# A graph-attention edge pass: the two weighted rows of a tile summed by an accumulating transfer instead of on VectorE

## The reference

```
xl = x @ Wl + bl;  xr = x @ Wr + br
e = leaky_relu(xl[src] + xr[dst], 0.2);  logits = sum over a head of e * att
m = segment_max(logits, dst);  p = exp(logits - m[dst]);  s = segment_sum(p, dst)
out = segment_sum(xl[src] * (p / s[dst]), dst) + bias      # self loops are added to src, dst
```

## Time and profile before

| | |
|---|---|
| device time, median of 3 | 3344.33 us |
| profiled execution: device time, span | 3327.99 us, 3326.3 us |
| busy in the span: PE, DVE, ACT, POOL | 82%, 85%, 51%, 25% |
| L732 of tile 0 to L677 of tile 75, pass 0 | 558.42 to 1105.00 us |
| mean granted TensorE clock | 0.916 of 2.4 GHz |

### The profile page before, as it was taken

How to read it: one execution, slowest core, us unless ns; L and a number is a source line. 1 busy time by engine, 2 the same in 40 slices (tenths; PEclk the granted TensorE clock), 3 DMA queues, 4 the chain that set the end, 5 groups by cost and what they waited for, 6 DMA issues and landing times. The chain is left out here.

```text
span 3326.3 us, 41230 instructions
## 1 busy us (share of the span) xinstructions
PE 2743.9 (82%) x11205; PEld 1838.8 (55%) x11205; DVE 2818.5 (85%) x5994; ACT 1689.0 (51%) x4291; POOL 844.1 (25%) x741
## 2 busy tenths in 40 slices
PE   7999997777777199999977777771899999688886
PEld 5777774333333078888843333330688888555554
DVE  7999996999999566767759999995988887399999
ACT  4545552555555433333315555553778787144443
POOL 0022212333332033333333333321333332000000
PEclk8999998889888589999988898885899999899998
DMA  9989997444443288887754444433999997388886
GB/s 322 344 300 318 319 335 268 133 153 150 152 154 121 72 271 274 271 266 261 251 198 142 150 152 155 149 105 131 379 357 351 350 345 269 129 292 287 293 291 226
DMA packets 332178, 788.76 MB, mean 237 GB/s; under 512 B 55070, under 2 KB 55616, under 8 KB 321738
## 3 DMA queue, kind: packets, MB, share of 16 engines
q1 hardware_dynamic: 265464, 622.14, 53.7%
q0 software_dynamic: 64032, 160.18, 15.1%
q10 hardware_dynamic: 2452, 3.79, 0.3%
HBM read 510.62 MB, written 329.28 MB: 253 GB/s over the span
## 5 line engine op out<-in xcount | busy, mean ns | idle before, releaser
L862 PE MATMUL bank<-wr,nT_e 128*128 128x512 f32 x1280 | 690.0, 689 | 241.7 <-ACT nT_e L662 241.4
L862 PEld LDWEIGHTS bank<-wr,nT_e 128*128 128x128 f32 x1280 | 268.5, 221 | 561.2 <-issue 292.3
L1019 PE MATMUL bank<-whi,t_hi 128*128 128x512 f32 x1256 | 525.1, 418 | 24.3 <-DVE t_lo L405 24.3
L1021 PE MATMUL bank<-whi,t_lo 128*128 128x512 f32 x1256 | 499.3, 398 | 0.0
L1020 PE MATMUL bank<-wlo,t_hi 128*128 128x512 f32 x1256 | 499.1, 397 | 0.0
L640 POOL DMA_INDIRECT nv_e<-rows,dst_row x160 | 255.6, 1598 | 701.8 <-ACT w_e L680 563.7
L677 ACT ACTIVATE w_e<-vs_e,ex_e 128x128 f32<-128x128 f32 x640 | 204.3, 390 | 336.3 <-DVE acc_e L794 251.6
L1019 PEld LDWEIGHTS bank<-whi,t_hi 128*128 128x128 f32 x1256 | 238.0, 189 | 74.6 <-issue 17.8
L1021 PEld LDWEIGHTS bank<-whi,t_lo 128*128 128x128 f32 x1256 | 238.1, 190 | 59.0
L1020 PEld LDWEIGHTS bank<-wlo,t_hi 128*128 128x128 f32 x1256 | 238.5, 190 | 45.1
L1209 PE MATMUL bank<-g_hi,whi 128*128 128x512 f32 (+1 forms) x640 | 263.0, 411 | 0.0
(11 more groups left out here) (244 smaller groups left out, 5852.9 us busy)
## 6 DMA issues: line engine op xcount, KB each, us to landing
rows<-t_row SPq DMA_DIRECT2D x312, 512.0 KB, 3.9
touched<-done_e SPq DMA_DIRECT2D x160, 256.0 KB, 2.0
xin<-in_x SPq DMA_DIRECT2D x156, 256.0 KB, 4.7
xTin<-in_xT SPq DMA_DIRECT2D x156, 256.0 KB, 3.5
vin<-rows SPq DMA_DIRECT2D x156, 256.0 KB, 4.0
g_vin<-rows SPq DMA_DIRECT2D x156, 256.0 KB, 5.7
g_xin<-in_x SPq DMA_DIRECT2D x156, 256.0 KB, 6.4
x_table<-g_shifted SPq DMA_DIRECT2D x156, 256.0 KB, 6.2
```

The costliest lines, as they stand in the source:

```text
L862: pe.matmul(psR[b][:, :], nT[:, b, cc, :], wr[:, cc, :], start=(cc == 0), stop=False)
L1019: pe.matmul(ps, hi[:, cc, :], whi[:, cc, :], start=(cc == 0), stop=False)
L1021: last = pe.matmul(ps, lo[:, cc, :], whi[:, cc, :], start=False, stop=(cc == KC - 1))
```

## The change

POOL now issues, for each tile, one more DMA: a transfer from SBUF to SBUF of `w2` onto `w1` (128 partitions of 2 KB), which adds to what stands there. DVE's addition L787 is gone, and accumulate waits for the transfer. `w1` and `w2` have four slots, the running sum comes two turns later (accumulate(k-8), scale(k-9)), the ring of gathers has 14 slots, and the transposes and their copies lead by one tile more. The fetched row and the joined row of the end of a pass share the slots 0 and 1 of `w1`; so the memset of the first moves from the start of the pass to its end.

```
-R = 12
+R = 14
+WR = 4
-        w1, w2 = sb("w1", [P, 2, D]), sb("w2", [P, 2, D])
+        w1, w2 = sb("w1", [P, WR, D]), sb("w2", [P, WR, D])
-        first_row, joined = sb("first_row", [P, D]), sb("joined", [P, D])
+        first_row, joined = w1[:, 0, :], w1[:, 1, :]
-            pipeline(T, [(gather, 0)])
+            def add_own(t):
+                b = t % WR
+                pool.wait_ge(s["weighted"], t + 1)
+                pool.dma_start(w1[:, b, :], w2[:, b, :], accum_op=ALU.add).then_inc(w_added[b], 16)
+
+            pipeline(T + G + 1, [(lambda t: add_own(t - G - 1) if t > G else None, 0),
+                                 (lambda t: gather(t) if t < T else None, 8)])
...
-                need(act, s["summed"], t - 1)
+                need(act, s["summed"], t - WR + 1)
...
-            lag = G + 2
-            pipeline(T + lag, [(lambda t: copy_transposed(t) if t < T else None, 1),
+            lag = G + 4
+            pipeline(T + lag, [(lambda t: copy_transposed(t) if t < T else None, 2),
...
-            dve.memset(first_row[:, :], 0.0).then_inc(s["cleared"], 1)
...
             def accumulate(t):
-                i, b = t // G, t % 2
-                dve.wait_ge(s["weighted"], t + 1)
-                dve.tensor_tensor(w1[:, b, :], w1[:, b, :], w2[:, b, :], ALU.add).then_inc(s["added"], 1)
-                dve.wait_ge(s["added"], t + 1)
+                i, b = t // G, t % WR
+                dve.wait_ge(w_added[b], w0 + 16 * (t // WR + 1))
                 need(dve, s["scaled"], t - AR + 1)
...
-            lag = G + 1
+            lag = G + 3
...
+            dve.wait_ge(s["summed"], T)
+            dve.memset(first_row, 0.0).then_inc(s["cleared"], 1)
...
-            pipeline(T, [(transposes, 2), (roots, 1)])
+            pipeline(T, [(transposes, 3), (roots, 1)])
```

More of the change, by code:

```diff
@@ L127, in build @@
         g["gathered_before"] = [0] * R
+        g["w_added"] = [ctx.enter_context(nc.semaphore(f"w_added{u}")) for u in range(WR)]
         for k in ("pads_stored", "dst_all_loaded", "scattered", "window_loaded", "row_fetched", "join_stored"):
@@ L601, in edge_pass @@
         best, gain, sums, scale4 = (sb(k, [P, H]) for k in ("best", "gain", "sums", "scale4"))
-        first_row, joined = sb("first_row", [P, D]), sb("joined", [P, D])
+        first_row, joined = w1[:, 0, :], w1[:, 1, :]
         s = group(nc, c, f"e{layer}", "w_loaded w_high w_low b_loaded chain ready transposed featT root z leaky product logit "
-                  "bottom exps cap ups left_over inverted weighted added summed scaled trail_set trail_stored others_loaded "
+                  "bottom exps cap ups left_over inverted weighted summed scaled trail_set trail_stored others_loaded "
                   "share_exps share_in share_T share_copied shared joined cleared",
@@ L608, in edge_pass @@
         got, got0 = g["gathered"], list(g["gathered_before"])
+        w_added, w0 = g["w_added"], layer * 16 * len(range(0, T, WR))
         for t in range(T):
@@ L648, in _ @@
                 pool.wait_ge(s["stored"][u], 16 * len(range(u, T, SR)))
-            pool.indirect_dma_start(first_row[:, :], None, touched[:, :],
+            pool.indirect_dma_start(first_row, None, touched[:, :],
                                     bass.IndirectOffsetOnAxis(g["join_row"][:, 0:1].bitcast(U32), 0),
@@ L653, in _ @@
             pool.indirect_dma_start(touched[:, :], bass.IndirectOffsetOnAxis(g["join_row"][:, 0:1].bitcast(U32), 0),
[L654 removed]
+                                    joined, None, bounds_check=P * T - 1, oob_is_err=False).then_inc(g["join_stored"], 16)
             pool.wait_ge(g["join_stored"], 16 * (layer + 1))
@@ L671, in weigh @@
             def weigh(t):
-                i, u, b = t // G, t % R, t % 2
+                i, u, b = t // G, t % R, t % WR
                 probs = ex[:, i % 2, 0:2 * H * G].rearrange("p (a h g) -> p a h g", a=2, h=H)
                 act.wait_ge(s["exps"], i + 1)
-                need(act, s["summed"], t - 1)
+                need(act, s["summed"], t - WR + 1)
                 for h in range(H):
```

## The result

| | before | changed |
|---|---|---|
| median of 4 runs | 3344.88 us (3344.17 to 3345.87) | 3244.7 us (3240.09 to 3246.64) |
| profiled execution: device time, span | 3327.99, 3326.3 us | 3245.37, 3243.6 us |
| mean granted TensorE clock | 0.916 | 0.932 of 2.4 GHz |

The ratio is 0.9698 [0.9682, 0.9715]: 100 us less, where 98 were forecast (3246 us).

A forecast was written before the change was run, and what follows sets the result against it. The prediction took DVE, busy 97% of pass 0's loop, as the bound. Per pass 52.4 + 1.3 + 2.0 - 3.5 - 2.8 - 0.4 = 49.0 us, 98 for two: 3344.3 - 98 = 3246 us, range 3236 to 3280.

The forecast's parts named there:

- The bound: Loop of pass 0: DVE is the full engine, busy 97%; what a tile costs DVE is what it takes.
- Loop, 52.4 + 1.3: DVE's loop, per pass: removed addition gains 52.4 us, two accumulations moved to the pass's end gain 1.3.
- the stall of 2.0: Turn 6 of each pass, behind the first exponentials: DVE's wait goes with the longer lead, gaining 2.0 us.
- Start, -3.5: Start of each pass: first multiplication waits for tile 2's gathers, costing 3.5 us, bounds 2.7 to 4.6.
- my extra for the clock: Start of each pass: PE's clock may rise later, lengthening the first multiplication by up to 0.9 us.
- End, -2.8 and -0.4: End of each pass: two more scalings and the last transfer cost 2.8 us, the moved memset 0.4.
- The cover: Loop: new work stays hidden in a 6.23 us turn; transfer takes 1.5 us of DMA engines, POOL's turn 4.2.
- (a): Loop: slow accumulating transfer lengthens the turn; 3523 us at 5 us of engine time a tile; chance 0.08.
- (b): Loop: POOL becomes the bound if the addition's issue takes over 2.6 us; 3342 us at 3.3; chance 0.03.
- (c): Loop: PE at its low clock bounds again; 3313 us if half the tiles are slow; chance 0.05.
- (d): Loop: DVE saves the addition but waits as long for the transfer or ACT; 3350 us; chance 0.02.
- I assume that offset stays: Sum: the runs' median, 16.3 us above the profiled execution, was taken to stay so after the change.

The follow-up runs named there:

- before_no_sum: The kernel before without DVE's addition L787 and nothing in its place, so the self loop's row is left out: 3242.24 us, ratio 0.9702.
- before_paced_2: The kernel before with start gathers paced (tile t from 6 to 11 waits for roots(t-6)), on the chip that stalls: 3328.83 us, ratio 0.9961.
- burst_of_ten: The changed kernel with ten gathers in the first burst, the eleventh waiting for roots(0), and so on: 3221.75 us, ratio 0.9685.
- delay_six: The changed kernel with the running sum at its old delay, accumulate(k-6) and scale(k-7): 3224.81 us, ratio 0.9692.
- two_transfers: The changed kernel with a second accumulating transfer per tile, into a row nobody reads: 3233.21 us, ratio 0.9717.
- no_pe_lead: The changed kernel with the transposes and their copies back at their old leads (2 and 1): 3252.27 us, ratio 0.9734.
- before_again: The kernel before, unchanged, run and profiled again: 3342.32 us, ratio 1.0001.
- six_and_paced: The changed kernel with accumulate(k-6) and the start gathers paced behind a burst of ten: 3238.22 us, ratio 0.969.

## Why the prediction was right

**The bound.** DVE at 97% of the loop before and after, and before_no_sum alone gives 102 us, with a turn of 6.24 us. Removing the one instruction was the whole of it.

**Loop, 52.4 + 1.3, and the stall of 2.0, per pass.** The turn came to 6.21 us (6.23 forecast). The stall of turn 6 is gone in the changed kernel; it stays in before_paced_2. From the first subtraction to tile 75's weighing there were 546.6 us in the profile before, and are 499.2 now, with 10.3 us of start stalls in them: 57.6 us gained without these, where the terms say 55.7. The 1.9 us more are the 0.1 us by which a group is shorter than forecast, 16 times, and rounding of starts.

**Start, -3.5.** The first gather to the first logits is 19.2 us, 16.75 before: -2.45 us in the profile. The transposes of tile 2 wait for its gathers as forecast (this pass begins 1.6 us earlier than in the earlier trace rows):

```profile
551.84 1.11 PE L862 MATMUL bank<-ident,nv_e 128*128 128x128 f32 x4 [0.84 <-DMA vs_e<-rows,src_row]
552.75 5.94 PE L870 MATMUL bank<-wr,nT_e 128*128 128x512 f32 x8
```

The multiplication is 5.94 us long, 0.23 more than in the earlier trace rows, not 0.9. It starts 0.91 us after the transposes, as in the earlier trace rows, where my sum took their whole 1.11. So my extra for the clock was too high, and 2.45 lies just under my low bound of 2.7.

**End, -2.8 and -0.4.** The end of pass 0 in the changed kernel:

```profile
1074.86 6.23 ACT L699 ACTIVATE done_e<-acc_e,inv_e 128x128 f32<-128x128 f32 x20
...
1075.27 0.87 POOL L651 DMA_DIRECT2D w_e<-w_e  x1 [2.64 <-ACT w_e L689]
...
1078.91 0.75 DVE L800 SCALAR_TENSOR_TENSOR acc_e<-acc_e,same,w_e 128x512 f32<-128x512 f32 x1 [3.10 <-DMA w_e<-w_e]
...
1085.26 0.48 DVE L820 MEMSET w_e<- 128x512 f32 x1
1085.66 0.11 DVE L821 COPY trail_e<-top_e 128x4 f32<-128x4 f32 x1
```

The scalings take 6.23 us where 12 instructions took 3.60: 2.6 us more, and the memset 0.4. The last sum (1079.7) is there before the scaling gets to it: the last transfer took 3.6 us from its issue to L800, where I took 4.1 from the gathers for the landing. The median was 3.7 in burst_of_ten. (The 3.4 that the expectation of delay_six names is not that of the transfers: it comes from the fetch and the store of the joined row, the only landings on that tile that the trace of the changed kernel tells.) The Trainium skill's fit (DMA: Bandwidth & Descriptors, "Anatomy of one DMA — SWDGE (gpsimd) path") gave 2.6 us as an estimate: it suits the plain copy (2.3) but not the accumulating one (3.7). Neither moved the end by more than 0.4.

**The cover.** The new transfer takes 0.61 x 6.21 - 0.352 x 6.94 = 1.35 us of the engines a tile (1.5 forecast; 61.0% and 35.2% are the queue's shares in 600 to 1060 after and before). POOL's turn is 0.98 + 1.02 + 1.03 + 0.9 = 3.9 us (4.2 forecast), by two errors that cancel: the accumulating issue takes 0.98 us, not 0.57, and the gather's 1.02, not 1.73, because L643 now begins at 789.70, after L745 with its two SBUF inputs has ended at 789.28. Where the issue still fell beside it, once in each pass, L643 took 1.83 us (604.16 and 1712.97). By the Trainium skill (SBUF — State Buffer, "Who interferes with whom") a VectorE instruction with two SBUF inputs contends with a GpSimd instruction that reads SBUF. The trace agrees for the gathers' issues, 1.83 us beside L745 and 1.02 after it. POOL's share in the middle is 49%; I had said 60% of the turn including gaps, and 3.9 of 6.21 is 63%.

**The rivals.** (a) and (b) are refuted by two_transfers: twice the price of the transfer and a POOL busy for 68% leave DVE at 97%. (c): the clock in the window 700 to 900 rose from 0.89 to 0.97 when the long wait gave way to short ones, and no_pe_lead, where the long wait is back, has 0.92. (d): the turn is what the missing instruction says.

**The sum.** In the profile the gain was 82.6 us, not 98. Its parts: 115.2 less (2 x 57.6), start -4.9, end -6.0 (2 x 3.0), stalls -20.2 make 84.1; 1.5 us stay unassigned. (The 57.6 and the 3.0 were read in pass 0 and are taken twice.) The timed runs gained 100 us because the kernel before stalls too in them, for about 14 us by before_again and before_paced_2. My step "I assume that offset stays" so was no explanation. The offset was mostly the stall, and it grew from 14 to 20 us. Without stalls the change is worth 105.5 to 106.0 us, not 98, since the loop and the start came out better than forecast. So two errors of 6 to 8 us nearly cancel: the sum was too low for the passes, and the growth of the stalls was missing from it. The forecast was right by its mechanism, and within 2 us by luck.

**What stays open.** Why one chip stalls and another doesn't, and whether the changed kernel itself would be free of it on the second; it wasn't run there, delay_six and burst_of_ten were. How the burst delays a count is open as well. The last late count tends to arrive as the burst ends: in ten of the twelve starts that stalled with the whole burst it came within 1 us of the last packet on POOL's queue (in the changed kernel 579.7 against 578.7, and 1688.5 against 1687.9). The amount of traffic alone doesn't say: in 551 to 590 the DMA share is 0.57 in the first profile of before (no stall) and 0.54 in before_again (stall).

## What to carry to other kernels

Price a removed VectorE instruction by the difference of starts, and ask whether its engine is full in that stretch; a transfer within SBUF can take over an addition, and is free in the loop as long as its engine time, its issue and its landing fit into the turn and the slots; here the longer delay around it cost 3 us at the end of each pass. Pace the first burst of gathers behind the consumer instead of issuing a whole ring at once: that one wait was worth 14 us before and 20 us after on a chip that stalls, and cost nothing where it doesn't. When a profile and the median of the runs differ, don't carry the difference along as a constant: take a second profile of the kernel before, on the chip of the comparison.

## What the runs showed of the hardware

- In a burst of 14 x 2 gathers from POOL, counts of PE that DVE and ACT wait for arrived 7 and 12 us after PE's instruction had ended (570.5 and 579.7 above); over all kernels that stalled it was 2 to 14 us. It happened with 12 tiles in the burst (before_again) and, for 10 us in place of 20, with ten (six_and_paced), and not with six. One chip showed it in both groups that ran there, another in neither of the two kernels that ran the whole burst there (delay_six, two_transfers), nor in the median of the kernel before.
- An accumulating transfer of 256 KB within SBUF takes 1.35 to 1.4 us of the 16 engines together, a plain copy about 0.5 (0.477 x 6.21 - 2.44, the gathers' part before); it lands in 3.7 us against 2.3; its issue takes 0.98 us of POOL against 0.57.
- The DMA engines could be busy to a share of 1.00 with the turn still 6.2 us; only the landing grew (medians of 4.8 us for the first transfer of a tile and 5.9 for the second, 8.3 at most).
